# A state-space layer's scan: a decay factor computed ahead into a borrowed bank, transposes for VectorE put first, and a residual sum moved to VectorE

## Chip, cores and metric

One core of a Trainium2 chip. The metric is the time of one execution of the whole kernel on the device, in microseconds (us); the figure compared is the median over runs.

## What is computed

The kernel is one layer with a Mamba-like mixer and a mixture of experts. Input x is 8 sequences of 1024 tokens with 256 channels; the mixer has 512 inner channels and 16 states per channel.

```python
u, res = split(x @ W_in); u = silu(conv3(u))
dt, B, C = split(u @ W_x)
delta = softplus(dt @ W_dt + b_dt)
h = exp(delta * A) * h + delta * u * B      # scan over tokens, 16 states
y = (sum over states of h * C) + u * D_param
x = layernorm(x + (y * silu(res)) @ W_out)
x = layernorm(x + ffn(x))                   # top-2 of 8 experts
```

The change touches the mixer and its layer norm alone. Everything is float32 there.

## The kernel before

**Tiling.** The mixer (`attention`) works in 16 chunks of 512 tokens, two to a sequence; chunk numbers below count from 0. Channels lie on the 128 partitions in 4 tiles (t), so a chunk has 16 states times 4 tiles = 64 **slots**, slot = 4n + t. In every slot ScalarE computes the decay factor `da` = exp(delta * A) for 128 x 512 into one of two PSUM banks (L428; t even to one, t odd to the other) and VectorE scans it with `dbu` (L534) into `hst`. GpSimd makes `dbu` = (delta u) times B for a whole state, 128 x 2048, once in four slots (L349), into one of three buffers. ScalarE writes `da` of a slot only once the scan two slots before is done, since it has two banks. Odd chunks, which continue a sequence, start each scan from `carry`.

**After the scan of a state** TensorE transposes it (`turn`, L619), 128 tokens at a time: token blocks 0 and 1 through the single bank `hd`, which VectorE multiplies by C and adds to `yacc` (`add_state`, L512), after the scans of t = 1 and t = 3; blocks 2 and 3 through the single bank `w2`, which ScalarE scales by C into `hTC` (`scale_state`, L416), and which TensorE transposes back into accumulation banks (`accumulate`, L628). All of this is done while the next state is scanned, part of it in the state after that. TensorE's order in the four slots of a state is: turn block 2, turn block 0, turn block 3, turn block 1, with accumulations after the second and the fourth (L655 to L662).

**The projections share one ring of two banks**, `gen`. A table, `FILL_AT`, gives each fill's bank and the slots at which TensorE writes its parts; `READ_AT` gives the slot at which ScalarE reads it. They are: `r` (gate, 4 fills of 2 parts), `u` (convolution, 4 of 6 parts), `xd`, `cT`, `d`, `ud` for the next chunk; `C`, `o`, `xt`, `lg` to close the chunk before. `o0` and `o1` are the output projection plus the residual: for two token blocks each, four products with `w_out` and a fifth with the identity that adds `x_rows` (L592, L594). ScalarE reads them into `resid` with a row sum beside (L401), then takes the squares' sum (`STATS_AT`, L479), GpSimd makes `rstd` and `shift` with small operations at n = 11 (L317 to L324), and ScalarE normalises at slots 45 to 49 (L488).

**Order.** Every engine's order is written out by hand in slots; each waits in its own order on counting semaphores. At slot 19 ScalarE runs `SILU_AT`: a table load, SiLU of `u` and of the gate (128 x 2048 each), and a load of the exp table (L451 to L454). GpSimd multiplies by the gate in two halves (`GATE_AT`, before `dbu` of n = 4 and of n = 5, L313); `o0` and `o1` wait for these. `o1` alone is written ahead of the slot's turn (`BEFORE_TURN`, slot 20). Stages -2, -1 and 16 of the same code fill and empty the pipeline: chunk 0 has nothing to close, chunk 15 has nothing of a next chunk to prepare, and stage 16 only closes.

After the mixer come routing, the experts and a last normalisation, in which VectorE takes row statistics with `bn_stats` (L1526) and `bn_aggr`.

## Time and profile before

| | us |
|---|---|
| median of 3 runs | 2740.91 |
| lowest, highest | 2738.28, 2741.33 |
| the profiled execution: time | 2734.82 |
| the profiled execution: span | 2733.0 |
| PE busy | 2380.6 (87%) |
| DVE busy | 2104.4 (77%) |
| POOL busy | 1796.5 (66%) |
| ACT busy | 1769.6 (65%) |

The span runs from the first to the last instruction. PE is TensorE (matmuls; PEld its weight loads), DVE VectorE, ACT ScalarE, POOL GpSimd, SP SyncE, which issues DMAs. The mixer's chunks fill the time from 87 to about 1802 us; the busy shares above are means over it and over the experts' part, in which TensorE and others have other limits. An engine's idle time counts only on the path that sets the end, so the chunks are read by themselves. Times in a timeline are from the span's start; in brackets stands the idle time before an instruction and what ended it.

### The profile page before, as it was taken

The page shows a single profiled execution, that of the slowest core. Times are in us where ns is not written, and L with a number is a line of the kernel's source. Part 1 is how long each engine was busy: PE and PEld are TensorE (multiplying, and loading weights), DVE is VectorE, ACT ScalarE, POOL GpSimd, SP SyncE. Part 2 cuts the span into 40 slices and gives each one's busy share as a digit, 9 for nine tenths or more (in the row PEclk, how much of TensorE's full clock was granted, in tenths as well). Part 3 has the DMA queues.
Part 4 walks back from the last instruction along what each step waited for, and adds up shares of the span by engine and source line. Part 5 has one row for each costly group of instructions (what it writes and reads, how often), then busy time and mean ns, then how long its engine had stood idle before and what let it go on. Part 6 is the DMA issues. An engine that isn't in the chain of part 4 may idle for free. (4 is left out here: it accounts for less than half of the span.)

```text
span 2733.0 us, 44490 instructions
## 1 busy us (share of the span) xinstructions
PE 2380.6 (87%) x14216; PEld 1854.8 (68%) x14216; DVE 2104.4 (77%) x2764; ACT 1769.6 (65%) x3135; POOL 1796.5 (66%) x845
## 2 busy tenths in 40 slices
PE   7799999999998999998999997654899999999991
PEld 2466666756666667566666665544799989989991
DVE  0698888988988988989889889958476567567644
ACT  3688878887887887888878888733243344334434
POOL 0787877887888789778788788822164345425524
PEclk9999999999999999999999999975899999999996
DMA  2111211121121111111212111120122221323116
GB/s 69 39 48 55 70 56 63 57 64 61 55 65 54 63 55 63 63 55 55 71 47 63 55 62 63 47 77 23 44 67 53 72 67 34 84 59 82 34 19 253
DMA packets 84393, 169.79 MB, mean 62 GB/s; under 512 B 8480, under 2 KB 52000, under 8 KB 84144
## 3 DMA queue, kind: packets, MB, share of 16 engines
q1 hardware_dynamic: 68784, 145.72, 15.7%
q0 software_dynamic: 15360, 20.98, 4.5%
q8 instruction: 128, 2.10, 0.3%
q14 instruction: 121, 0.99, 0.1%
HBM read 130.49 MB, written 36.18 MB: 61 GB/s over the span
## 5 line engine op out<-in xcount | busy, mean ns | idle before, releaser
L349 POOL TENSOR_TENSOR dbu<-du,b_all 128x2048 f32<-128x2048 f32 x256 | 1161.7, 4545 | 166.4 <-DVE hst L534 166.3
L428 ACT ACTIVATE da<-delta,a_neg 128x512 f32<-128x512 f32 x1024 | 705.7, 691 | 255.6 <-DVE hst L534 249.4
L534 DVE TENSOR_TENSOR_SCAN hst<-da,dbu 128x512 f32<-128x512 f32 x512 | 600.3, 1207 | 131.6 <-ACT da L428 129.1
L534 DVE TENSOR_TENSOR_SCAN hst<-da,carry,dbu 128x512 f32<-128x512 f32 x512 | 630.8, 1267 | 53.6 <-ACT da L428 49.0
L619 PEld LDWEIGHTS w<-ident,hst 128*128 128x128 f32 x2048 | 232.5, 141 | 417.9 <-ACT hTC L416 270.0
L619 PE MATMUL w<-ident,hst 128*128 128x128 f32 x2048 | 324.4, 281 | 193.8 <-ACT hTC L416 166.6
L1424 PE MATMUL gu<-x_part,w_part 128*128 128x384 f32 (+1 forms) x2304 | 485.6, 359 | 4.9 <-ACT w_part L1320 3.2
L1424 PEld LDWEIGHTS gu<-x_part,w_part 128*128 128x128 f32 x2304 | 403.5, 189 | 35.3 <-DVE silu L1278 3.6
L512 DVE SCALAR_TENSOR_TENSOR yacc<-hd,c_tok,yacc 128x512 f32<-128x512 f32 x512 | 374.8, 732 | 66.0 <-PE hd L619 64.2
L557 PE MATMUL gen<-xT,w_u 128*128 128x512 f32 x768 | 394.3, 604 | 14.3 <-DVE w_u L497 12.7
L416 ACT ACTIVATE hTC<-w,c_tok 128x512 f32<-128x512 f32 x512 | 346.0, 676 | 9.1 <-PE w L619 9.1
L1361 ACT ACTIVATE silu<-gu 128x384 f32<-128x384 f32 (+1 forms) x192 | 101.3, 528 | 374.6 <-PE gu L1424 374.6
L619 PEld LDWEIGHTS hd<-ident,hst 128*128 128x128 f32 x2048 | 247.0, 142 | 137.6 <-issue 126.4
L1278 DVE TENSOR_TENSOR silu<-silu,gu 128x384 f32<-128x384 f32 (+1 forms) x192 | 114.5, 596 | 270.3 <-ACT silu L1361 267.9
L619 PE MATMUL hd<-ident,hst 128*128 128x128 f32 x2048 | 314.0, 276 | 0.7
L628 PE MATMUL acc<-ident,hTC 128*128 128x128 f32 x2048 | 310.0, 274 | 0.0
L1156 POOL DMA_INDIRECT xg<-x_dram,token x80 | 83.5, 1043 | 277.9 <-DVE token L1227 255.9
L1441 PE MATMUL dn<-w_part,hid_part 128*128 128x256 f32 x1920 | 257.9, 281 | 4.9 <-ACT eo L1340 4.9
L1441 PEld LDWEIGHTS dn<-w_part,hid_part 128*128 128x128 f32 x1920 | 251.3, 188 | 12.8 <-ACT eo L1340 6.8
L628 PEld LDWEIGHTS acc<-ident,hTC 128*128 128x128 f32 x2048 | 242.2, 142 | 0.0
L1151 POOL TENSOR_TENSOR w_part<-w_raw,w_mask 128x512 fp32r<-128x512 f32 x84 | 119.7, 1526 | 109.5 <-DVE w_mask L1242 109.5
L1166 POOL DMA_INDIRECT acc_dram<-eo,token x80 | 128.4, 1605 | 74.9 <-issue 42.4
(197 smaller groups left out, 2913.2 us busy)
## 6 DMA issues: line engine op xcount, KB each, us to landing
b_all<-b_rows SPq DMA_DIRECT2D x128, 512.0 KB, 3.6
xT<-in_xT SPq DMA_DIRECT2D x16, 514.0 KB, 4.9
x_rows<-in_x SPq DMA_DIRECT2D x16, 512.0 KB, 4.9
x_dram<-x SPq DMA_DIRECT2D x16, 512.0 KB, 3.1
acc_dram<-x SPq DMA_DIRECT2D x16, 512.0 KB, 5.1
w_raw<-in_wg SPq DMA_DIRECT2D x8, 1024.0 KB, 5.0
w_raw<-in_wu SPq DMA_DIRECT2D x8, 1024.0 KB, 8.0
w_raw<-in_wd SPq DMA_DIRECT2D x8, 1024.0 KB, 12.5
```

The lines of the kernel that those rows point to most:

```text
L349: nc.gpsimd.tensor_tensor(dbu[DBU[n]][:], du[parity][:], b_n, ALU.mult).then_inc(dbu_ready, 1)
L416: nc.scalar.activation(hTC[(2 * n + i) % 4][:], w2_bank[:], ACT.Copy, scale=c_tok[parity][:, LB + i, RANK + NST + n:RANK + NST + n + 1]).t ...
L428: nc.scalar.activation(da_bank[t % 2][:], delta[parity][:, t, :], ACT.Exp, scale=a_neg[:, t, n:n + 1]).then_inc(da_ready, 1)
L512: nc.vector.scalar_tensor_tensor(out=yacc[parity][:, l, :], in0=hd_bank[:], scalar=c_tok[parity][:, l, RANK + NST + n:RANK + NST + n + 1], ...
L534: nc.vector.tensor_tensor_scan(hst[DBU[n]][:, t, :], da_bank[t % 2][:], dbu[DBU[n]][:, t, :], initial, ALU.mult, ALU.add).then_inc(scanned, 1)
L557: last = nc.tensor.matmul(bank[:], w_u[:, tap, k, j * P:(j + 1) * P], xT[:, k, tap:tap + CL], start=part == 0, stop=part == parts - 1)
L619: last = nc.tensor.transpose(bank[:, t * P:(t + 1) * P], hst[DBU[n]][:, t, l * P:(l + 1) * P], ident[:])
L628: last = nc.tensor.matmul(acc_bank[i][:, t, :], hTC[(2 * n + i) % 4][:, t * P:(t + 1) * P], ident[:], start=False, stop=n == NST - 1, is_t ...
L1151: nc.gpsimd.tensor_tensor(parts[1], raw, mask_of(w, p, F32), ALU.subtract).then_inc(w_low, 1)
L1166: nc.gpsimd.indirect_dma_start(out=acc_d, out_offset=bass.IndirectOffsetOnAxis(ap=token[par][:, s:s + 1], axis=0), in_=eo[:, s, :], in_off ...
L1424: last = nc.tensor.matmul(gu_bank[n % 2][i][:, 0:width(n)], gu_part[wp][:, i, kk, f * P:(f + 1) * P], x_part[xp][:, kk, tokens_of(j)], sta ...
L1441: last = nc.tensor.matmul(dn_bank[s // SJ][:, s % SJ, :], hid_part[hp][:, h % HS, s * P:(s + 1) * P], down_part[wp][:, f, :], start=f == 0 ...
```

## The change

- **The early factor.** `da` of slot 20 is computed by ScalarE at slot 17, behind its other work there, into ring bank 1 instead of an own bank; VectorE scans slot 20 out of that bank. `da` of slot 22 then waits for the scan of slot 18 alone.
- **Ring bank 1** is free for it because `o1` is moved from slot 20 to slots 21 and 22, behind the turns and behind the scan of slot 20; the first part of `u0` goes from slot 24 to slot 25.
- **Turn order.** TensorE turns blocks 0, 2, 1, 3 (for state 4: 0, 1, 2, 3) instead of 2, 0, 3, 1. ScalarE's scalings, and with them the seeds and reads of the accumulation banks, go a slot or two later; both accumulations now come a state later, after the second and the fourth turn. VectorE's check that `hst` is free is now on block 3 (`w2_ready`).
- **`o0` goes to VectorE.** TensorE leaves out the two identity products for it; VectorE adds `x_rows` to the bank (blocks 2, 3), takes `bn_stats` and `bn_aggr`. This, and both `add_state` of state 4, stand behind the scan of slot 20. ScalarE no longer reads `o0` nor squares its blocks; `o1`'s stay, with statistics at slot 25.
- **GpSimd** has six small operations at n = 11 instead of four; its gate multiplies go to n = 5 and n = 6. The load of `x_rows` waits for `shift_ready` instead of the read of `o1`.

```diff
+VECTOR_READ = ("o0",)
+EARLY_SLOT, EARLY_AT, EARLY_BANK, EARLY_STATE = 20, 17, 1, 4
...
-           "o0": (0, 14, 15, 16, 17, 18), "o1": (1, 20, 20, 20, 20, 20), "xd": (0, 22, 23, 24, 25),
-           "u0": (1, 24, 25, 26, 27, 29, 30), ...
+           "o0": (0, 14, 15, 16, 17), "o1": (1, 21, 21, 21, 22, 22), "xd": (0, 22, 23, 24, 25),
+           "u0": (1, 25, 26, 27, 29, 30, 30), ...
...
-BEFORE_TURN = ("o1",)
+BEFORE_TURN = ()
-SEED_AT, ACC_READ_AT = (6, 8), (5, 7)
-SILU_AT, STATS_AT, EXP_AT, LN_AT, NORM_AT = 19, (22, 24), (41, 42), (43, 44), (45, 46, 48, 49)
-GATE_AT, SMALL_AT, ADD_AT, DU_AT = {4: 1, 5: 0}, 11, 14, 15
+SEED_AT, ACC_READ_AT = (8, 10), (7, 9)
+SILU_AT, STATS_AT, EXP_AT, LN_AT, NORM_AT = 19, 25, (41, 42), (43, 44), (45, 46, 48, 49)
+GATE_AT, SMALL_AT, ADD_AT, DU_AT = {5: 1, 6: 0}, 11, 14, 15
...
+        late = [x for x in same if FILL_AT[x][1] > EARLY_SLOT]
+        if self.main and FILL_AT[name][0] == EARLY_BANK and name == late[0]:
+            pe.wait_ge(scanned, self.c * SLOTS + EARLY_SLOT + 1)
...
+    def da_bank_free(self, slot):
+        return self.c * SLOTS + slot - (3 if slot == EARLY_SLOT + 2 else 1)
...
                         if s.close:
-                            sp.wait_ge(ring_read, o1_read)
+                            sp.wait_ge(shift_ready, shifted)
...
-                        wait_over(act, scanned, c * 64 + slot - 1)
-                        nc.scalar.activation(da_bank[t % 2][:], delta[parity][:, t, :], ACT.Exp,
-                                             scale=a_neg[:, t, n:n + 1]).then_inc(da_ready, 1)
-                    if t == 2 and s.state_before(n, 1) is not None:
+                        if slot != EARLY_SLOT:
+                            wait_over(act, scanned, s.da_bank_free(slot))
+                            nc.scalar.activation(da_bank[t % 2][:], delta[parity][:, t, :], ACT.Exp,
+                                                 scale=a_neg[:, t, n:n + 1]).then_inc(da_ready, 1)
+                    if t == 3 and s.state_before(n, 1) is not None:
...
-                    if t == 0 and s.state_before(n, 2) is not None:
+                    if t == 1 and s.state_before(n, 2) is not None:
...
+                    if slot == EARLY_AT and s.main:
+                        en, et = EARLY_SLOT // DT, EARLY_SLOT % DT
+                        wait_over(act, ring_read, s.early_bank_free())
+                        nc.scalar.activation(gen_bank[EARLY_BANK][:], delta[parity][:, et, :], ACT.Exp,
+                                             scale=a_neg[:, et, en:en + 1]).then_inc(da_ready, 1)
...
+            def sum_rows(s):
+                dve.wait_ge(rows_loaded, c * 16)
+                dve.wait_ge(ring_full, s.nth_full("o0") + 1)
+                wait_over(dve, x1_ready, c * LT - LT)
+                for l in O_BLOCKS[0]:
+                    nc.vector.tensor_tensor(resid[:, l, :], gen_bank[FILL_AT["o0"][0]][:, l % 2 * DM:(l % 2 + 1) * DM],
+                                            x_rows[:, l, :], ALU.add).then_inc(rows_summed, 1)
+            def measure_rows(s):
+                dve.wait_ge(rows_summed, c * 2)
+                for l in O_BLOCKS[0]:
+                    nc.vector.bn_stats(stats[:, l - 2, :], resid[:, l, :]).then_inc(rows_measured, 1)
...
-                        dve.wait_ge(da_ready, c * 64 + slot + 1)
+                        dve.wait_ge(da_ready, c * 64 + DA_ORDER.index(slot) + 1)
...
-                                dve.wait_ge(hd_ready, c * (NST * LB) + LB * done + LB)
+                                dve.wait_ge(w2_ready, c * (NST * LB) + LB * done + LB)
...
-                    if t % 2 == 1 and s.state_before(n, 1) is not None:
+                    if t % 2 == 1 and n != EARLY_STATE + 1 and s.state_before(n, 1) is not None:
                         add_state(s, s.state_before(n, 1), t // 2)
+                    if slot == EARLY_SLOT:
+                        if s.main:
+                            add_state(s, s.state_before(n, 1), 0)
+                        if s.close:
+                            sum_rows(s)
+                            measure_rows(s)
+                            dve.wait_ge(rows_measured, c * 2)
+                            wait_over(dve, shift_ready, c - 1)
+                        if s.main:
+                            add_state(s, s.state_before(n, 1), 1)
+                        if s.close:
+                            aggregate_rows(s)
...
-                        turn(one, (2, 0, 3, 1)[q])
-                    if q == 1 and two is not None:
-                        accumulate(two, 1)
-                    if q == 3 and one is not None:
-                        accumulate(one, 0)
+                        turn(one, ((0, 1, 2, 3) if n == EARLY_STATE + 1 else (0, 2, 1, 3))[q])
+                    if q % 2 == 1 and two is not None:
+                        accumulate(two, q // 2)
```

## Rows read from the trace of the kernel before

**Rows 1.** Stretches, chunk 6 and all: us, busy PE PEld DVE ACT POOL, PEclk, DMA, GB/s.

```profile
733.36:841.79 108.43, 98.34 (x576) 68.95 (x575) 94.41 (x97) 88.98 (x154) 91.01 (x40) 1.00 0.19 60
86.98:1805.00 1718.02, 1521.38 (x9000) 1081.81 (x8998) 1534.78 (x1536) 1396.64 (x2390) 1398.99 (x504) 0.99 0.18 58
```

**Rows 2.** VectorE's waits: who waited, for whom, us in total, times, longest.

```profile
DVE hst L534 <- ACT da L428: 178.1, 85, 71.1
...
DVE yacc L512 <- PE hd L619: 64.2, 99, 1.9
```

**Rows 3.** Timeline of VectorE in chunk 6, slots 18 to 36: start, us, engine, line.

```profile
759.60 2.32 DVE L534 TENSOR_TENSOR_SCAN hst<-da,dbu 128x512 f32<-128x512 f32 x2
...
761.85 0.72 DVE L512 SCALAR_TENSOR_TENSOR yacc<-hd,c_tok,yacc 128x512 f32<-128x512 f32 x1
...
767.16 2.34 DVE L534 TENSOR_TENSOR_SCAN hst<-da,dbu 128x512 f32<-128x512 f32 x2 [4.59 <-ACT da L428]
...
771.83 1.22 DVE L534 TENSOR_TENSOR_SCAN hst<-da,dbu 128x512 f32<-128x512 f32 x1 [0.56 <-ACT da L428]
...
777.05 0.75 DVE L512 SCALAR_TENSOR_TENSOR yacc<-hd,c_tok,yacc 128x512 f32<-128x512 f32 x1 [0.27 <-PE hd L619]
...
781.18 0.75 DVE L512 SCALAR_TENSOR_TENSOR yacc<-hd,c_tok,yacc 128x512 f32<-128x512 f32 x1 [1.14 <-PE hd L619]
...
788.22 2.33 DVE L534 TENSOR_TENSOR_SCAN hst<-da,dbu 128x512 f32<-128x512 f32 x2
...
794.49 2.34 DVE L534 TENSOR_TENSOR_SCAN hst<-da,dbu 128x512 f32<-128x512 f32 x2 [0.41 <-POOL carry L346]
```

**Rows 4.** Timeline of ScalarE in chunk 6, slots 19 and 20.

```profile
759.86 1.28 ACT L451 ACT_TABLE_LOAD   x1
...
766.18 0.69 ACT L428 ACTIVATE da<-delta,a_neg 128x512 f32<-128x512 f32 x1
766.81 0.67 ACT L416 ACTIVATE hTC<-w,c_tok 128x512 f32<-128x512 f32 x1
```

**Rows 5.** Groups by line and form: ScalarE's reads and squares, VectorE's nearest kinds.

```profile
L401 ACT ACTIVATE resid<-gen 128x256 f32<-128x256 f32 x64 | 23.3, 369 | 10.0 <-PE gen L594 10.0
...
L479 ACT ACTIVATE x<-resid,minus_mean 128x256 f32<-128x256 f32 x64 | 32.0, 501 | 1.0
...
L1278 DVE TENSOR_TENSOR silu<-silu,gu 128x512 f32<-128x512 f32 x64 | 43.9, 686 | 103.1 <-ACT silu L1361 102.5
...
L1526 DVE BATCH_NORM_STATS2 stats<-rows 128x6 f32<-128x256 f32 x64 | 23.2, 404 | 19.3 <-DMA rows<-acc_dram 19.3
```

**Rows 6.** Timeline of TensorE in chunk 6, slot 20.

```profile
761.70 1.89 PE L592 MATMUL gen<-w_out,yT 128*128 128x256 f32 x8
...
763.43 0.59 PE L594 MATMUL gen<-x_rows,ident 128*128 128x256 f32 x2
...
767.53 0.66 PE L619 MATMUL w<-ident,hst 128*128 128x128 f32 x4 [1.35 <-ACT hTC L416]
768.02 0.60 PE L619 MATMUL hd<-ident,hst 128*128 128x128 f32 x4
```

**Rows 7.** Timeline of GpSimd in chunk 6, the multiply for n = 6.

```profile
760.62 4.57 POOL L349 TENSOR_TENSOR dbu<-du,b_all 128x2048 f32<-128x2048 f32 x1
```

**Rows 8.** Timeline of VectorE in chunk 6, slots 59 and 61.

```profile
832.82 0.75 DVE L512 SCALAR_TENSOR_TENSOR yacc<-hd,c_tok,yacc 128x512 f32<-128x512 f32 x1 [0.84 <-PE hd L619]
...
836.82 0.75 DVE L512 SCALAR_TENSOR_TENSOR yacc<-hd,c_tok,yacc 128x512 f32<-128x512 f32 x1 [1.00 <-PE hd L619]
```

**Rows 9.** Timeline of VectorE in chunk 5, slot 3.

```profile
630.87 0.75 DVE L512 SCALAR_TENSOR_TENSOR yacc<-hd,c_tok,yacc 128x512 f32<-128x512 f32 x1 [0.79 <-PE hd L619]
```

**Rows 10.** Timeline of VectorE in chunk 15, slot 21.

```profile
1733.71 0.75 DVE L512 SCALAR_TENSOR_TENSOR yacc<-hd,c_tok,yacc 128x512 f32<-128x512 f32 x1 [1.92 <-PE hd L619]
```

**Rows 11.** Timeline of VectorE and GpSimd in the last normalisation.

```profile
2698.42 0.72 DVE L1526 BATCH_NORM_STATS2 stats<-rows 128x6 f32<-128x256 f32 x2
2698.66 0.55 POOL L1557 TENSOR_SCALAR rows<-rows,rstd,shift 128x256 f32<-128x256 f32 x1
```

More of the change, by code:

```diff
@@ L82, in nth_full, with base_read, wait_bank, early_bank_free @@
         return self.base() + sorted(self.fills, key=lambda x: FILL_AT[x][-1]).index(name)
+    def base_read(self):
+        k = len(VECTOR_READ)
+        if not isinstance(self.c, int):
+            return self.c * (len(FILL_AT) - k) + (36 - len(FILL_AT) + k)
+        return self.base() - max(0, self.c - 1) * k
     def nth_read(self, name):
-        return self.base() + sorted(self.fills, key=lambda x: READ_AT[x]).index(name)
-    def read_before(self, name):
+        read = [x for x in self.fills if x not in VECTOR_READ]
+        return self.base_read() + sorted(read, key=lambda x: READ_AT[x]).index(name)
+    def wait_bank(self, pe, name, ring_read, rows_summed, scanned):
         same = [x for x in self.fills if FILL_AT[x][0] == FILL_AT[name][0]]
         k = same.index(name)
-        return self.nth_read(same[k - 1]) + 1 if k else self.base()
+        if k and same[k - 1] in VECTOR_READ:
+            pe.wait_ge(rows_summed, self.c * 2)
+        else:
+            wait_over(pe, ring_read, self.nth_read(same[k - 1]) + 1 if k else self.base_read())
+        late = [x for x in same if FILL_AT[x][1] > EARLY_SLOT]
+        if self.main and FILL_AT[name][0] == EARLY_BANK and name == late[0]:
+            pe.wait_ge(scanned, self.c * SLOTS + EARLY_SLOT + 1)
+    def early_bank_free(self):
+        used = [x for x in self.fills if FILL_AT[x][0] == EARLY_BANK and x in READ_AT and READ_AT[x] <= EARLY_AT]
+        return self.nth_read(max(used, key=lambda x: READ_AT[x])) + 1 if used else self.base_read()
+    def da_bank_free(self, slot):
+        return self.c * SLOTS + slot - (3 if slot == EARLY_SLOT + 2 else 1)
     def state_before(self, n, back):
@@ L207, in attention @@
         gated = sem("gated")
+        rows_summed = sem("rows_summed")
+        rows_measured = sem("rows_measured")
+        moments_ready = sem("moments_ready")
         mean_ready = sem("mean_ready")
@@ L467, in chunk @@
                                              ).then_inc(soft_step, 1)
-                    if slot in STATS_AT and s.close:
-                        j = STATS_AT.index(slot)
-                        act.wait_ge(ring_read, s.nth_read(f"o{j}") + 1)
-                        if j == 0:
-                            wait_over(act, x1_stored, c * 32 - 32)
-                        pair = slice(O_BLOCKS[j][0], O_BLOCKS[j][-1] + 1)
+                    if slot == STATS_AT and s.close:
+                        act.wait_ge(ring_read, s.nth_read("o1") + 1)
+                        wait_over(act, x1_stored, c * 32 - 32)
+                        pair = slice(O_BLOCKS[1][0], O_BLOCKS[1][-1] + 1)
                         nc.scalar.activation(minus_mean[:, pair], row_sum[:, pair], ACT.Copy,
                                              scale=-1.0 / DM).then_inc(mean_ready, 1)
-                        act.wait_ge(mean_ready, c * 2 + (j - 1))
-                        for l in O_BLOCKS[j]:
+                        act.wait_ge(mean_ready, c)
+                        for l in O_BLOCKS[1]:
                             last = nc.scalar.activation(x1[:, l, :], resid[:, l, :], ACT.Square,
@@ L515, in add_state, with aggregate_rows @@
                     in1=yacc[parity][:, l, :], op0=ALU.mult, op1=ALU.add).then_inc(summed, 1)
+            def sum_rows(s):
+                c = s.c
+                dve.wait_ge(rows_loaded, c * 16)
[5 more added lines that the diff above has]
+            def measure_rows(s):
+                c = s.c
+                dve.wait_ge(rows_summed, c * 2)
+                for l in O_BLOCKS[0]:
+                    nc.vector.bn_stats(stats[:, l - 2, :], resid[:, l, :]).then_inc(rows_measured, 1)
+            def aggregate_rows(s):
+                for l in O_BLOCKS[0]:
+                    nc.vector.bn_aggr(mean_var[:, l - 2, :], stats[:, l - 2, :]).then_inc(moments_ready, 1)
             def chunk(s):
@@ L533, in chunk @@
                         initial = carry[:, n, t:t + 1] if parity == 1 else 0.0
[L534 removed]
+                        decay = gen_bank[EARLY_BANK] if slot == EARLY_SLOT else da_bank[t % 2]
+                        nc.vector.tensor_tensor_scan(hst[DBU[n]][:, t, :], decay[:], dbu[DBU[n]][:, t, :],
                                                      initial, ALU.mult, ALU.add).then_inc(scanned, 1)
[L536 removed]
+                    if t % 2 == 1 and n != EARLY_STATE + 1 and s.state_before(n, 1) is not None:
                         add_state(s, s.state_before(n, 1), t // 2)
+                    if slot == EARLY_SLOT:
[10 more added lines that the diff above has]
+                            aggregate_rows(s)
             over_chunks(dve, chunk)
@@ L550, in fill @@
                 if part == 0:
-                    wait_over(pe, ring_read, s.read_before(name))
+                    s.wait_bank(pe, name, ring_read, rows_summed, scanned)
                 what, j = name.rstrip("0123"), int(name[-1]) if name[-1].isdigit() else 0
@@ L585, in fill @@
                         pe.wait_ge(gated, c * 2 + (j - 1))
-                    if name == "o0" and part == 0:
+                    if name == "o1" and part == 0:
                         pe.wait_ge(rows_loaded, c * 16)
-                    for l, t in [(l, t) for l in O_BLOCKS[j] for t in range(DT + 1)][2 * part:2 * part + 2]:
+                    terms = DT if name in VECTOR_READ else DT + 1
+                    for l, t in [(l, t) for l in O_BLOCKS[j] for t in range(terms)][2 * part:2 * part + 2]:
                         acc = bank[:, l % 2 * DM:(l % 2 + 1) * DM]
                         if t < DT:
-                            nc.tensor.matmul(acc, yT[:, t, l * P:(l + 1) * P], w_out[:, t, :], start=t == 0, stop=False)
+                            last = nc.tensor.matmul(acc, yT[:, t, l * P:(l + 1) * P], w_out[:, t, :], start=t == 0,
+                                                    stop=t == terms - 1)
                         else:
```

30 lines of the change are left out of this document (19 added, 11 removed), and 2 rows, old and new, of the table FILL_AT.

## The prediction

> **What bounds the kernel now.** I read the stretches first. Over the mixer's chunks VectorE is busy 1534.8 of 1718 us; in chunk 6, which I take as the pattern, 94.4 of 108.4 us, GpSimd 91.0, ScalarE 89.0 and TensorE 98.3, whose ends are modelled [rows 1]. Four engines are nearly full, and VectorE's scans carry the order, so what counts is VectorE's idle time: 14.0 us a chunk. Its waits name two causes: decay factors (178.1 us in 85 waits, 71.1 of it the one before the first scan, so 107 in the chunks) and the transposed state in `hd` (64.2 us in 99) [rows 2]. The timeline shows where. The pair of slots 18 and 19 starts at 759.60, its `add_state` at 761.85, and slot 20 only at 767.16, after 4.59 us for its factor; then come smaller waits for factors (0.56) and, as TensorE has fallen behind, for `hd` (0.27, 1.14) [rows 3]. ScalarE's timeline gives the reason: from the load of the SiLU table at 759.86 to the next factor at 766.18 it is 6.32 us in the SiLU block [rows 4]. The two banks hold factors for two slots, 2.3 us of scans.
>
> **The change, part by part,** walked through chunk 6, on its clock.
>
> *ScalarE into the block.* The extra Exp at slot 17 costs 0.63 (766.18 to 766.81 [rows 4]); I price it at nothing, since ScalarE then waits for scan 16 anyway; were it busy there, 0.63. The scaling moved from slot 18 to slot 19, 0.57, lies ahead of the block. So the block starts at about 760.43, and the next factor, now slot 21's, starts 6.32 later, 766.75, and is ready at 767.4.
>
> *VectorE in that time.* The last `add_state` frees it at 762.5. Slot 20 has its factor: 1.2, to 763.7. First `add_state` of state 4, 0.65. Two adds of 128x256 from PSUM: no row shows them; half of a 128x512 one (0.69) is 0.34, a whole one the upper end [rows 5]; I take 0.38 as overhead doesn't halve, 0.75 together. Two `bn_stats`, 0.72 for two back to back [rows 11], 0.40 each by the mean [rows 5]: 0.72. Second `add_state` 0.65. Two aggregations, no row here: between nothing and a `bn_stats` each; 0.2 together. Hand-overs of VectorE to itself: 0.2. End 766.9 (766.4 to 768.2 at the bounds). Slot 21 waits 0.5 and starts at 767.45. The new work of 1.9 us lies wholly beside the block; without the block it would cost 1.9.
>
> *Slots 21 to 27.* Scans 21, 22, 23 follow at 1.15 each with factors in time, as ScalarE has lost the reads of `o0` (0.37 each and accumulator reads) and two squares (0.50 each) [rows 5], 2.6 us with their small companions. Slot 24 starts at 771.0; before, the factor of slot 23 alone came at 771.83 [rows 3]. Now `o1` presses: TensorE wrote it in the shadow from 761.70; four of its products take 1.73 (761.70 to 763.43), so 0.43 each and 4.3 in all [rows 6]. Now it starts behind the second turn, at 765.3 (`add_state` ends 764.3, a turn and an accumulation under 0.49 each: 767.53 to 768.02, after a wait [rows 6]), has 6 products done at 767.9, waits for ScalarE's scaling (768.1), and is full at 770.3. ScalarE reads it and takes its statistics between the factors of slots 24, 25 and 26: VectorE waits 0.45 and 0.65. Then slots 26, 27 and an `add_state`: slot 28 starts at 778.0. Before, the wait of 1.14 ended at 781.18, and slot 28 followed at 781.85 [rows 3]. `o0` without its two identity products saves TensorE 0.86.
>
> *Slots 28 to 35.* TensorE has the rest of `u0`, `cT` and `d0` and is a turn ahead of what it was, because `hd` now comes first. By its sum (a convolution part, 512 columns, twice a 256-column product: 0.86; a turn 0.44, my estimate for one that runs on, below the 0.49 above) `hd` for slot 33 comes at 787.5 while VectorE is there at 786.5: a wait of 1.0. Slot 32 starts at 784.2 (before 788.22), slot 36 at 791.2 (before 794.49, behind a wait of 0.41) [rows 3]. **Gain to here 3.3 us**, of 7.7 that slots 20 to 31 waited.
>
> *Slots 36 to 63.* ScalarE is full from slot 38 to 49 (softplus, normalisation); the order of scalings changes, the sum doesn't: +0.4. From slot 46 TensorE is full with `u2`, `u3`, `ud`, `xt` and `lg`. The waits for `hd` at slots 59 and 61, 0.84 and 1.00 [rows 8], and two or three small ones go, 2.7 us, as the turns for VectorE come a slot sooner. In return slot 60 waits for the last turn of state 13 in `w2` at TensorE's slot 59 (this is the new check; nothing but that scan is queued behind it): 0.55 by my sum, and 0.2 elsewhere. **Gain 2.0 and 0.4.** At the start of odd chunks the wait of 0.79 [rows 9] goes, 0.4 on average.
>
> *Priced at nothing.* GpSimd's gate multiplies a state later: the multiply for n = 6 runs to 765.2 [rows 7], and slot 24 comes at 771; `o0`'s start at slot 14 gets its gate 0.1 before its turn (0.5 if I read that wrong). GpSimd's two added small operations, at most the 0.55 of a larger one each [rows 11], lie in an idle stretch of it before n = 12. The load of `x_rows` is held on SP's queue till GpSimd's small operations at n = 11; behind it stands only the load of B for n = 14, which waits for the multiply of n = 11 anyway.
>
> *Sum.* A chunk: 3.3 + 0.4 + 2.0 + 0.4 = 6.1. The walk leaves out small hand-overs (0.04 to 0.1 each, some nine): I take **5.2** for each of chunks 1 to 14, 73 us. Chunk 0 has the block but no `o`: 4. Chunk 15 has no block: 1.9 of new work, against a wait of 1.92 for `hd` behind `o1` [rows 10], which goes: nothing. The closing stage saves the identity products, 1. Sum 78. The profiled execution, 2734.8 (1.8 above its span), would become 2657; the median of the runs lies 6.1 above it, so 2663.
>
> **A rule against the change.** In the last normalisation two `bn_stats` beside a GpSimd operation on SBUF (0.55 us) take 0.72 [rows 11], so 0.36 each, no more than the mean of all [rows 5]. The Trainium skill, SBUF — State Buffer, section "SBUF: two separate sides", says that VectorE in a two-port mode or with two SBUF inputs and GpSimd lock a shared port pair, and the loser waits for the whole instruction. By that rule `bn_stats` would only be held if it ran in such a mode, and the trace speaks against it. As a mechanism here: GpSimd's multiply from 760.62 runs to 765.19 [rows 7] and the next follows at once; `bn_stats` at 765.1 and its second would each wait out a 4.55 us multiply, 9 us less the 0.5 of slack: a loss of some 3 us a chunk.
>
> **Rivals.**
> - *TensorE takes over.* Its 98 us of busy time [rows 1] leave little; `o1`'s 4.3 us move out of the idle shadow into the stretch where it is behind. If that stretch and slot 60 lose another 2.2 us, 3 remain: 42 + 3 = 45 us, **2696**. For it: `hd` waits already stand there. Against: ScalarE's late scaling held it before (1.35 [rows 6]), and that no longer delays `hd`. 17%.
> - *The hand-written order was looser than I take it,* VectorE near its floor: idle outside the new waits gone, 7 us a chunk, 98 + 5: **2638**. 13%.
> - *Slower:* the place is slot 21. If `o1` counts whole (4.3), the new VectorE work counts whole (1.9) and the checks on `w2` at slots 60 and 4 cost one turn and one convolution part each (2.6), 8.8 stand against 7.2 recovered (4.59, 0.56, 0.27, 1.14 and some): +1.6 times 14, **2763**. It decides if less than 4.59 of the block is covered. 4%. The port lock, +3 times 15, gives 2786: 2%.
> - *The early factor doesn't come early:* scan 18 now waits for it too (20 factors counted). If ring bank 1 is not free at slot 17, the block's wait only moves; what is left is the turn order, some 2 us: **2710**. `r3` is read two slots before, so hardly. 4%.
>
> **Numbers.** My forecast has 60%, 2663; its own range is 2645 to 2685. To leave out no more than 2 in 10 the range is 2638 to 2700: it takes in TensorE's case and the better one. A difference below 0.2%, 5.5 us, can't be told here. Faster 0.92, same 0.02 (between the cases), slower 0.06.
>
> **What would show it.** `da` for slot 20 before that of slot 18; slot 20 without wait; 0.4 to 0.9 us before slot 21; `bn_stats` at 0.36; `hd` waits in total below 25 us; a wait of about 0.5 before slot 60; chunk 6 about 103 us long. Wrong would be: `bn_stats` over 1 us, a wait before slot 20, `hd` waits of over 2 us in slots 26 to 35, or the wait at slot 60 over 1.5.

## The result, and the profile after

The changed kernel took **2718.09 us**, median of four runs (2715.93 to 2720.49), against 2741.12 for four runs of the kernel before (2738.28 to 2741.41): a ratio of 0.9918 [0.9906, 0.9930]. It is 23 us faster. The forecast was 78 us, and its range ended at 2700: the sign came true, the size did not.

The profiled execution took 2720.49 us, span 2718.7. The profile splits it at two rows of VectorE's timeline: the first scan of chunk 0, and the maximum over the router's logits, where the mixer is over. The first fence is the kernel after, the second the kernel before.

```profile
88.33 2.34 DVE L599 TENSOR_TENSOR_SCAN hst<-da,dbu 128x512 f32<-128x512 f32 x2 [72.51 <-ACT da L467]
...
1811.93 0.69 DVE L1023 TENSOR_REDUCE row_max<-logits 128x64 f32<-128x512 f32 x1 [16.89 <-PEq L149]
```

```profile
1830.39 0.69 DVE L947 TENSOR_REDUCE row_max<-logits 128x64 f32<-128x512 f32 x1 [28.53 <-PEq L123]
```

Before, the mixer took 1743.4 us (1830.39 less the start at 86.98, the first stretch of [rows 1]), after 1723.6: 19.8 us less, where 78 were forecast. Chunks 1 to 14 gained 20.8 us, 1.5 each instead of 5.2; chunk 0 lost 0.6, chunk 15 and the closing stage 0.4. What follows, the experts' part, ran 902.6 us before and 906.8 after in the profiled executions, though its code is the same. The profiled execution of before lay 6.3 below its median, so the medians differ by more than the two profiles do; for the mixer I go by the profiles, for the whole by the medians.

Chunk 6 in the stretches, and VectorE's waits over the whole program (for [rows 1] and [rows 2]):

```profile
728.59:836.08 107.49, 99.52 (x572) 69.75 (x572) 96.53 (x103) 88.12 (x145) 92.03 (x42) 0.98 0.19 60
```

```profile
DVE hst L599 <- ACT da L467: 142.1, 120, 72.5
...
DVE yacc L554 <- PE hd L697: 47.2, 58, 1.7
```

VectorE has 2.1 us more work in the chunk (96.5 against 94.4 [rows 1]) and is idle 11.0 instead of 14.0. The granted clock of the chunk is 0.98 instead of 1.00. The waits for factors fell by 36 us in all, those for `hd` by 17; they were to fall below 25. VectorE's timeline tells which went and which came (slots 20 to 37; before in [rows 3]):

```profile
757.45 1.23 DVE L599 TENSOR_TENSOR_SCAN hst<-gen,dbu 128x512 f32<-128x512 f32 x1
...
759.23 0.76 DVE L566 TENSOR_TENSOR resid<-gen,x_rows 128x256 f32<-128x256 f32 x2
760.02 0.75 DVE L574 BATCH_NORM_STATS2 row_stats<-resid 128x6 f32<-128x256 f32 x2
760.97 0.75 DVE L554 SCALAR_TENSOR_TENSOR yacc<-hd,c_tok,yacc 128x512 f32<-128x512 f32 x1 [0.20 <-DVE row_stats L574]
761.64 0.24 DVE L579 BATCH_NORM_AGGREGATE row_mean_var<-row_stats 128x2 f32<-128x6 f32 x2
762.41 3.53 DVE L599 TENSOR_TENSOR_SCAN hst<-da,dbu 128x512 f32<-128x512 f32 x3 [0.54 <-ACT da L467]
766.86 1.22 DVE L599 TENSOR_TENSOR_SCAN hst<-da,dbu 128x512 f32<-128x512 f32 x1 [0.92 <-ACT da L467]
768.40 1.22 DVE L599 TENSOR_TENSOR_SCAN hst<-da,dbu 128x512 f32<-128x512 f32 x1 [0.32 <-ACT da L467]
770.62 0.75 DVE L554 SCALAR_TENSOR_TENSOR yacc<-hd,c_tok,yacc 128x512 f32<-128x512 f32 x1 [1.00 <-PE hd L697]
...
775.03 0.75 DVE L554 SCALAR_TENSOR_TENSOR yacc<-hd,c_tok,yacc 128x512 f32<-128x512 f32 x1 [1.41 <-PE hd L697]
775.70 2.33 DVE L599 TENSOR_TENSOR_SCAN hst<-da,dbu 128x512 f32<-128x512 f32 x2
...
784.41 1.22 DVE L599 TENSOR_TENSOR_SCAN hst<-da,dbu 128x512 f32<-128x512 f32 x1 [1.13 <-ACT da L467]
...
786.92 2.34 DVE L599 TENSOR_TENSOR_SCAN hst<-da,dbu 128x512 f32<-128x512 f32 x2 [0.45 <-ACT da L467]
...
790.14 2.34 DVE L599 TENSOR_TENSOR_SCAN hst<-da,dbu 128x512 f32<-128x512 f32 x2 [0.23 <-ACT da L467]
```

Slot 20 comes without a wait, the new work follows it, and slot 21 waits 0.54. Chunk 6 began at 733.36 before and at 728.59 now, so 4.77 is added to read these times on the clock of the prediction. The start of a slot, forecast and measured: 21: 767.45 and 767.18; 24: 771.0 and 771.63; 28: 778.0 and 780.47; 36: 791.2 and 794.91 (794.49 before). To slot 24 the walk holds within 0.6 us. From there on another 3.1 us are lost against it, in the waits of 0.32, 1.00 and 1.41 at slots 25 to 27 and in 1.13, 0.45 and 0.23 at slots 33, 34 and 36.

What TensorE did meanwhile (slots 20 to 24; before in [rows 6]), and the stretches around it, where the granted clock is the third column from the end:

```profile
757.61 0.66 PE L697 MATMUL hd<-ident,hst 128*128 128x128 f32 x4 [0.55 <-DVE yacc L554]
759.38 0.66 PE L697 MATMUL hd<-ident,hst 128*128 128x128 f32 x4 [1.12 <-DVE yacc L554]
759.87 0.73 PE L706 MATMUL acc<-ident,hTC 128*128 128x128 f32 x4
760.39 3.49 PE L669 MATMUL gen<-w_out,yT 128*128 128x256 f32 x8
...
766.84 1.06 PE L642 MATMUL gen<-u,w_x 128*48 128x512 f32 x2
```

```profile
757.00:759.00 2.00, 0.71 (x5) 0.42 (x4) 2.00 (x3) 2.00 (x2) 2.00 (x1) 1.00 0.87 186
759.00:760.40 1.40, 1.02 (x9) 1.02 (x10) 1.36 (x5) 1.38 (x2) 1.40 (x1) 0.93 0.00 0
760.40:762.00 1.60, 1.60 (x5) 1.33 (x5) 1.28 (x5) 1.59 (x2) 1.60 (x3) 0.50 0.00 0
762.00:764.20 2.20, 2.20 (x8) 1.76 (x8) 1.79 (x2) 2.10 (x4) 2.20 (x1) 0.63 0.00 0
764.20:766.00 1.80, 1.80 (x12) 1.60 (x11) 1.74 (x2) 0.87 (x3) 0.88 (x1) 1.00 0.00 0
```

With `o1` gone from the shadow of the block, TensorE waits 0.55 and 1.12 us for VectorE; from 757 to 759 it is busy 0.71 of 2.00 us. Then the granted clock is 0.50, 1.2 instead of 2.4 GHz, for some 3.4 us by these stretches, and it is there that `o1` is written: its first four products, eight instructions, take 3.49 us, where before four took 1.89 at the full clock [rows 6]. Eight chunks of the kernel after (1, 2, 4, 6, 7, 12, 13, 15) have this at slot 20. Of the closing chunks of the kernel before none has. The idle time alone does not settle it: chunk 8 of the kernel after has the same two waits, and stayed at the full clock.

```profile
974.11 0.66 PE L697 MATMUL hd<-ident,hst 128*128 128x128 f32 x4 [1.12 <-DVE yacc L554]
...
975.04 1.89 PE L669 MATMUL gen<-w_out,yT 128*128 128x256 f32 x8
```

```profile
971.74:973.74 2.00, 0.70 (x5) 0.42 (x4) 2.00 (x3) 2.00 (x2) 2.00 (x1) 1.00 0.56 156
...
975.14:976.74 1.60, 1.60 (x9) 1.42 (x8) 1.27 (x5) 1.59 (x2) 1.60 (x3) 1.00 0.00 0
```

Counted from their own start, both chunks reach slot 23 within 0.01 us of each other; chunk 8 reaches slot 24 sooner by 1.0 and slot 36 by 1.5. Against the kernel before it gains 1.07 us to slot 36, where chunk 6 loses 0.42: that is the price of one half clock.

The waits at slots 33 and 34 are read on ScalarE and TensorE:

```profile
783.20 0.60 ACT L409 ACTIVATE u_raw<-gen 128x512 f32<-128x512 f32 x1 [2.02 <-PE gen L634]
783.69 0.69 ACT L467 ACTIVATE da<-delta,a_neg 128x512 f32<-128x512 f32 x1
```

```profile
781.20 1.88 PE L634 MATMUL gen<-xT,w_u 128*128 128x512 f32 x4
```

ScalarE takes its work in order. It stands 2.02 us at its read of `u0`, whose last parts TensorE does only at 781.20 to 783.1, and the factor for slot 33 is queued behind that read. Chunk 14 has no `u0`, and ran at the full clock at slot 20: there the gain over the kernel before, counted from the chunk's start, is 3.0 us at slot 24, 2.15 at slot 28 and 2.16 at slot 36, and 3.15 at its end. In chunk 6 the same points give 1.98, 1.38, -0.42 and 0.94.

### The profile page after: what moved, and what is told of

Its sections match the earlier page's. It is cut to its first block and busy times, and to the rows that moved or that the text cites. A ratio compares the mean times of both kernels' runs of the same rounds, so it can differ in the third digit from the quotient of the medians.

```text
span 2718.7 us, 44389 instructions
## 1 busy us (share of the span) xinstructions
PE 2395.2 (88%) x14152; PEld 1856.4 (68%) x14152; DVE 2138.2 (79%) x2860; ACT 1757.7 (65%) x2991; POOL 1801.6 (66%) x877
## 3 DMA queue, kind: packets, MB, share of 16 engines
q14 instruction: 131, 1.07, 0.1%
## 5 line engine op out<-in xcount | busy, mean ns | idle before, releaser
L467 ACT ACTIVATE da<-delta,a_neg 128x512 f32<-128x512 f32 x1008 | 689.3, 691 | 132.4 <-DVE hst L599 118.0
L599 DVE TENSOR_TENSOR_SCAN hst<-da,dbu 128x512 f32<-128x512 f32 x504 | 592.5, 1212 | 110.2 <-ACT da L467 108.3
L599 DVE TENSOR_TENSOR_SCAN hst<-da,carry,dbu 128x512 f32<-128x512 f32 x504 | 621.1, 1271 | 39.9 <-ACT da L467 33.7
L697 PEld LDWEIGHTS hd<-ident,hst 128*128 128x128 f32 x2048 | 238.5, 142 | 328.1 <-DVE yacc L554 156.8
L697 PE MATMUL hd<-ident,hst 128*128 128x128 f32 x2048 | 323.5, 281 | 124.2 <-DVE yacc L554 105.6
L554 DVE SCALAR_TENSOR_TENSOR yacc<-hd,c_tok,yacc 128x512 f32<-128x512 f32 x512 | 375.9, 734 | 52.3 <-PE hd L697 47.2
L697 PEld LDWEIGHTS w<-ident,hst 128*128 128x128 f32 x2048 | 240.8, 143 | 208.0 <-ACT hTC L454 104.1
```

Of the source, the lines that this page charges most:

```text
L467: nc.scalar.activation(da_bank[t % 2][:], delta[parity][:, t, :], ACT.Exp, scale=a_neg[:, t, n:n + 1]).then_inc(da_ready, 1)
L554: nc.vector.scalar_tensor_tensor(out=yacc[parity][:, l, :], in0=hd_bank[:], scalar=c_tok[parity][:, l, RANK + NST + n:RANK + NST + n + 1], ...
L599: nc.vector.tensor_tensor_scan(hst[DBU[n]][:, t, :], decay[:], dbu[DBU[n]][:, t, :], initial, ALU.mult, ALU.add).then_inc(scanned, 1)
L697: last = nc.tensor.transpose(bank[:, t * P:(t + 1) * P], hst[DBU[n]][:, t, l * P:(l + 1) * P], ident[:])
```

## The experiments

"Mixer" is, as above, the time from the first scan to the maximum over the logits, from the profiled execution; the gain in a chunk is against the kernel before from the chunk's start on. The first group is four kernels; the kernel before took 2740.26 us beside them (13 runs), beside the second group 2742.33 (7), and beside the third, when the experts' part of every profiled kernel was some 36 to 40 us longer, 2778.83 (13). So across groups I compare ratios and mixers. Each mixer time comes from one execution, and the mean granted clock of the kernel after lay between 0.954 and 0.957 in its four runs, so a difference of a few us between two mixers is weak evidence by itself. The gains at a slot of chunk 6 repeat to a few hundredths wherever the clock is the same.

| kernel | median us | ratio to before | mixer us |
|---|---|---|---|
| after | 2718.09 | 0.9918 [0.9906, 0.9930] | 1723.6 |
| e1_zeros | 2719.76 | 0.9929 [0.9912, 0.9945] | 1713.3 |
| e2_o1first | 2710.50 | 0.9893 [0.9877, 0.9910] | 1713.4 |
| e3_o1cut | 2694.44 | 0.9828 [0.9812, 0.9844] | 1699.0 |
| e4_order | 2734.07 | 0.9979 [0.9970, 0.9989] | 1737.6 |
| e5_due | 2702.67 | 0.9855 [0.9839, 0.9872] | 1708.5 |
| e6_early | 2720.17 | 0.9919 [0.9902, 0.9935] | 1724.0 |
| e7_unroll | 2685.79 | 0.9795 [0.9778, 0.9811] | 1692.4 |
| e8_spread | 2700.50 | 0.9850 [0.9834, 0.9867] | 1702.2 |
| e9_before_unroll | 2761.80 | 0.9938 [0.9921, 0.9955] | 1730.2 |
| e10_spread_unroll | 2711.30 | 0.9757 [0.9740, 0.9773] | 1677.9 |
| e11_o1late | 2777.48 | 0.9988 [0.9977, 0.9999] | 1746.7 |
| e12_stats | 2751.61 | 0.9903 [0.9886, 0.9919] | 1720.0 |

### e1: TensorE kept busy in the shadow

In slot 20 of chunks 0 to 14, four products with zeros ahead of the first turn and ten behind it, added to a bank that they don't change.

```diff
+def fill_time(s, count):
+    for _ in range(count):
+        nc.tensor.matmul(acc_bank[1][:, 0, :], zeros[:], ident[:], start=False, stop=False,
+                         is_transpose=True, skip_group_check=True)
...
+if slot == EARLY_SLOT and s.main and s.front:
+    fill_time(s, 4)
 turn(one, ...)
```

> The changed kernel (2718 us) with 14 transposes of a zero tile, added to an accumulation bank, in the two places of slot 20 where TensorE stood idle (4 ahead of the first turn, 10 behind it); the results are the same. Theory A, the granted clock: in the changed kernel TensorE works at 0.50 to 0.63 for 3.4 us behind these idle places, just where o1 is written, and is the bound up to slot 33; with the filler the half clock goes, slots 21 to 33 shorten by 1.0 to 1.7 us a chunk, 2695 to 2704 us. Rival B, only the place of o1 counts and its end is covered by ScalarE: the clock comes back to 1.00 and the time stays at 2715 to 2720. Rival C: the filler delays the second turn and with it slot 21: over 2722.

The half clock at slot 20 was gone from all closing chunks (from chunk 15 too, which has no added products), and the mixer took 10.3 us less, with more work on TensorE than before the edit. In chunk 6 the gain at slot 36 rose from -0.42 to 1.06, what chunk 8 has without the edit. The time of the whole did not follow: the experts' part took 913.1 us instead of 906.8, and the median stayed at 2719.76. So the time alone would read as rival B, and theory A's 2695 to 2704 was missed; the mixer speaks for A's mechanism. The half clock was a cost of the change; it was not the largest.

### e2: a first part of o1 ahead of the turn

```diff
-BEFORE_TURN = ()
+BEFORE_TURN = (("o1", 0),)
```

(the part named is issued before the turn of its slot, the other four behind, as in the change)

> The changed kernel with the first of o1's five parts written ahead of the second turn of slot 21, in TensorE's idle time, the rest behind it. Theory A: o1 ends 0.9 us sooner by place, and if the shorter idle time also keeps the clock, 1.7 more; 2692 to 2708 us. Rival B (o1's end is covered): 2718. Rival C: the second turn comes some 0.3 us later and slot 21 with it: 2720 to 2724.

The same 10.2 us of the mixer, without the added work, and here 7.6 of them show in the time: 2710.50, just above theory A's range. In chunk 6 every start of a scan is that of e1 within 0.02 us, so the earlier place of the first part brought nothing there beyond the clock. Only chunks 1 and 13 still had the half clock at slot 20. Chunk 6 starts 5.7 us sooner here, so the stretch that was at 0.50 lies at about 755 to 758.5, and the clock is 1.00:

```profile
753.00:757.00 4.00, 3.73 (x20) 3.02 (x20) 3.22 (x9) 3.97 (x4) 4.00 (x3) 1.00 0.04 15
757.00:759.00 2.00, 1.67 (x10) 1.55 (x11) 2.00 (x2) 1.90 (x4) 2.00 (x1) 1.00 0.00 0
```

The gain in chunk 6 is 2.99 at slot 24, close to the forecast's 3.3 at slot 36; but 0.90 at slot 34. So a second loss lies behind.

### e3: a smaller o1

```diff
 for l, t in [(l, t) for l in O_BLOCKS[j] for t in range(terms)][2 * part:2 * part + 2]:
+    if name == "o1" and 0 < t < DT:
+        continue
```

> The changed kernel without six of the ten products of o1 (terms 1 to 3 of both blocks), so the output projection of two token blocks is incomplete. It prices TensorE's time in slots 21 to 33. If TensorE is the bound there, as theory A has it, 2.6 us at full clock and more at half come off each chunk until another engine takes over: 2675 to 2690 us. If ScalarE or VectorE is the bound there (rival B): 2712 to 2718.

With six products (2.6 us) of `o1` left out the mixer took 24.6 us less than after, 14.4 less than e2; the time, 2694.44, is 4 us above theory A's range. The gain at slot 28 is 4.17, where e2 has 2.87. So TensorE's work in slots 21 to 27 is on the path, and half of what is taken off it there comes back. (It was on the path before the change too, by the waits of 0.27 and 1.14 for `hd` [rows 3].) Yet the loss of 2 us between slots 32 and 34 is the same:

```profile
769.93 1.22 DVE L599 TENSOR_TENSOR_SCAN hst<-da,dbu 128x512 f32<-128x512 f32 x1 [1.13 <-ACT da L467]
...
772.45 2.34 DVE L599 TENSOR_TENSOR_SCAN hst<-da,dbu 128x512 f32<-128x512 f32 x2 [0.45 <-ACT da L467]
```

A TensorE that is 2.6 us less loaded in front of slot 28 leaves this wait at 1.13 and 0.45, to the hundredth. So it does not come from `o1`; the next pair of runs moves `u0`.

### e4 and e6: the change in steps

e4 is the kernel before with the new order of turns, scalings and gates alone; e6 adds the early factor to it, with the later places of `o1` and `u0`, and leaves `o0` as it was, read by ScalarE, with its identity products.

```diff
-SEED_AT, ACC_READ_AT = (6, 8), (5, 7)
+SEED_AT, ACC_READ_AT = (8, 10), (7, 9)
...
-turn(one, (2, 0, 3, 1)[q])
+turn(one, (0, 2, 1, 3)[q])
...
-if q == 1 and two is not None:
-    accumulate(two, 1)
-if q == 3 and one is not None:
-    accumulate(one, 0)
+if q % 2 == 1 and two is not None:
+    accumulate(two, q // 2)
```

> The kernel before (2741 us) with the turn order, the scalings, accumulations, seeds, gate multiplies and the check on w2 of the change, and nothing else: no early factor, o0 still with ScalarE. By the prediction's terms (2.4 us in slots 46 to 63, 0.4 at the chunk's start): 2700 to 2705 us. By the two traces (2.2 gained late, some 0.7 lost at the hand-over between chunks): about 2720. Rival: the order alone gives nothing, 2738 to 2744.

> The kernel of e4_order (2734 us) with the early factor, o1 at slots 21 and 22 and u0 a slot later, so the change without the move of o0 to VectorE: ScalarE still reads o0 and squares its blocks, TensorE still adds its rows. Theory A: the early factor moves o1 into TensorE's full stretch and ScalarE is loaded as before, so most of what is gained at slot 20 is lost by slot 34; 2722 to 2732 us, and the move of o0 is worth the rest to 2718. Rival: the early factor carries all of the gain, 2715 to 2721.

The order alone is worth 5.8 us of the mixer (its ten runs lie between 2729 and 2740, between its two cases), the early factor 13.6 more, and `o0` on VectorE 0.4. That last part saved ScalarE 2.0 us a chunk (the two reads and two squares of `o0`, 767.99 to 768.71 and 769.89 to 771.13 before) and TensorE 0.86, and brought nothing by itself. But e6 has the half clock in slot 20 of no closing chunk; on TensorE it differs from the kernel after by the identity products of `o0` (0.86 us), and of the two waits of chunk 6 at slot 20 it has only the second, 1.02. In e1 and e2, where `o0` is on VectorE and the clock stays up, the mixer is 10.7 and 10.6 us below e6. So this part of the change is worth about 10 us and gave them back, by the clock as far as e1 and e2 show.

### e5 and e8: u0 later

Both build on e2. e5 does the last part of `u0` a slot later and reads it a slot later, and moves the `d` blocks by a slot too:

```diff
-"u0": (1, 25, 26, 27, 29, 30, 30), "cT": (0, 28), "d0": (0, 31), "d1": (1, 33), "d2": (0, 35),
+"u0": (1, 25, 26, 27, 29, 30, 31), "cT": (0, 28), "d0": (0, 32), "d1": (1, 34), "d2": (0, 36),
```

e8 spreads `u0` among the `d` blocks and reads it at slot 36 instead of 32:

```diff
-"u0": (1, 25, 26, 27, 29, 30, 30), "cT": (0, 28), "d0": (0, 31), "d1": (1, 33), "d2": (0, 35),
+"u0": (1, 25, 27, 29, 30, 32, 34), "cT": (0, 28), "d0": (0, 31), "d1": (0, 33), "d2": (0, 35),
```

> The kernel of e2_o1first (2710.5 us) with the last part of u0 at slot 31 instead of twice at slot 30, its read at slot 33, and d0 to d3 filled a slot later (32, 34, 36, 38; d0 and d1 read at 34 and 36). In chunk 6 of the changed kernel ScalarE stands 2.02 us for the end of u0 and VectorE then 1.13 and 0.45 us for the factors of slots 33 and 34. Theory A (TensorE is full there, the read only shows it): the wait moves a slot on, at most 0.5 us a chunk gained, 2703 to 2712 us. Rival D (the two parts at slot 30 and the early read are the cause themselves): 1.0 to 1.5 us a chunk, 2689 to 2697 us.

> The kernel of e2_o1first (2710.5 us) with the parts of u0 spread over slots 25 to 34 and read at slot 36, d1 moved to bank 0 at slot 33. TensorE's work is the same, but less of it lies in slots 25 to 32 and more where TensorE stands idle behind slot 33. Theory A (TensorE is the bound in slots 25 to 33 alone): the waits for hd at slots 25 and 27 stay (0.95, 1.41), those of 1.13 and 0.45 at slots 33 and 34 go: 2688 to 2700 us. If ScalarE is the bound behind slot 33: 2705 to 2711.

e5 took 4.9 us off e2's mixer, and its time lies at the edge of theory A: in chunk 6 the gain at slot 34 rose from 0.90 to 2.54, and of the wait a part, 0.86, moved on to slot 35. e8 took 11.2 off. Slot 33 now follows slot 32 without a wait, and what is left stands at slots 34 and 36 (the rows are slots 32, 34 and 36 with the one behind each):

```profile
768.60 2.32 DVE L599 TENSOR_TENSOR_SCAN hst<-da,dbu 128x512 f32<-128x512 f32 x2
...
772.41 2.34 DVE L599 TENSOR_TENSOR_SCAN hst<-da,dbu 128x512 f32<-128x512 f32 x2 [0.53 <-ACT da L467]
...
775.97 2.34 DVE L599 TENSOR_TENSOR_SCAN hst<-da,dbu 128x512 f32<-128x512 f32 x2 [0.58 <-ACT da L467]
```

In the time e8 stands at 2700.50, 10 us below e2. So the second loss is the place of `u0`, which reaches VectorE by ScalarE's read of it ahead of a factor. Chunk 14, which has no `u0`, shows no loss there either. Both runs move TensorE's parts together with the read, so what the later read alone would give was not tried.

### e7 and e9: no loop over the chunks

A third loss lies at the start of odd chunks, where the loop's body begins anew. VectorE waits there before slot 0 and, in chunk 5, again at slots 3 and 4 ([rows 9] has the one at slot 3 before):

```profile
621.58 2.46 DVE L599 TENSOR_TENSOR_SCAN hst<-da,carry,dbu 128x512 f32<-128x512 f32 x2 [2.02 <-ACT da L467]
...
627.96 0.75 DVE L554 SCALAR_TENSOR_TENSOR yacc<-hd,c_tok,yacc 128x512 f32<-128x512 f32 x1 [0.92 <-PE hd L697]
629.42 2.46 DVE L599 TENSOR_TENSOR_SCAN hst<-da,carry,dbu 128x512 f32<-128x512 f32 x2 [0.70 <-PE w L697]
```

Both kernels have the chunks of the loop written out, e7 the one after, e9 the one before.

```diff
-with eng.Fori(0, (CHUNKS - 4) // 2) as i:
-    emit(Stage(i * 2 + 1, 1, True, True, True, True))
-    emit(Stage(i * 2 + 2, 0, True, True, True, True))
+for c in range(1, CHUNKS - 3):
+    emit(Stage(c, c % 2, True, True, True, True))
```

> The changed kernel (2718 us) with the twelve chunks of its loop written out, same instructions, no branch. In the trace VectorE waits 1.9 to 2.0 us at slot 0 of every second chunk (1.34 before the change), and TensorE's half clock stands at these places too. Theory E: the branch costs VectorE these 2 us six times and the half clock behind it another 1.6 in some: 2695 to 2706 us. Rival: the wait is for the state's last scalings, not for the branch; 2715 to 2718.

> The kernel before (2741 us) with the same twelve chunks written out. Written out, the changed kernel fell by 32 us, to 2685.8. Theory E1: the loop cost both kernels about the same, then this one falls by 20 to 30 us, 2711 to 2721, and the change is worth about as much without the loop as with it, 25 to 35 us. Rival E2: the change had made the branch dearer (ScalarE's last scaling now stands right ahead of it, the check on w2 behind it); then this one falls by 5 to 15 us only, 2726 to 2736, and the change without the loop is worth 40 to 50.

The loop costs the kernel before 13.2 us of its mixer and the kernel after 31.2. Without loops the change is worth 37.8 us of the mixer (1730.2 to 1692.4), with them 19.8, near the lower end of rival E2's 40 to 50. With the loop VectorE waits at slot 0 of chunks 3, 5, 7, 9 and 11, 1.17 to 1.34 us before and 1.87 to 2.10 after; written out, at slot 0 of none, in e7 and in e9. In e7 the start of chunk 7 runs through (slot 0 is the second row):

```profile
818.98 0.72 DVE L553 SCALAR_TENSOR_TENSOR yacc<-hd,c_tok,yacc 128x512 f32<-128x512 f32 x1
819.63 2.45 DVE L598 TENSOR_TENSOR_SCAN hst<-da,carry,dbu 128x512 f32<-128x512 f32 x2
```

e7 also has the half clock at slot 20 only in chunks 1, 9 and 15 instead of eight, which by e1 and e2 is some 7 of these 31 us. Of the remainder, 24 us, the five waits at slot 0 are 10.0 (6.3 before); the rest was not traced wait by wait. The half clock at slot 0 or 1 of chunks 3, 5 and 9 stands in the kernel before as well; the kernel after has it in chunk 11 too, for 6.8 us. In e4, which has the new order and no early factor, the waits at slot 0 are 2.03 to 2.54 already: it is the order that makes them longer. By what engine was not tried.

### e10: both

e8 with the chunks written out.

> e8_spread (2700.5 us) with the twelve chunks written out. If the gains add up (32 us for the loop, of which some 8 were half clock that e8 had lost already): 2666 to 2678 us. Rival: they overlap, as both take the same waits away: 2680 to 2686.

The mixer is 1677.9 us, 65.5 less than that of the kernel before, and the ratio 0.9757 [0.9740, 0.9773]: some 67 us, faster than both kernels; against 2741 that ratio is 2674, within the range for gains that add up. Chunk 6 has gained 2.63 us at slot 36 (e8: 2.36), 4.49 at slot 63 (4.29) and 5.88 at its end, where e8 has 3.45 and e7 4.87. Against e9, the kernel before without the loop, it is 52.3 us of the mixer.

### e11: o1 spread over eight slots

As e10, but `o1` at slots 21 to 29 and read at 31, `u0` wholly behind it at 31 to 36, and all four `d` blocks in one bank.

> Written out, and o1's five parts spread over slots 21, 23, 25, 27, 29 (read at 31), u0 behind it at slots 31 to 36 (read at 38), xd and d all in bank 0. It takes TensorE's work out of slots 21 to 30, where theory A has it as the bound, and puts it into slots 31 to 38, where TensorE waits. Theory A: the waits of 0.95 and 1.41 us for hd at slots 25 and 27 go, another 1.0 to 2.0 us a chunk: 2645 to 2660 us. Rival: ScalarE, with the same reads later, or u1 behind d3 in bank 0 gives it back: 2665 to 2680.

A miss: the mixer took 1746.7 us, 68.8 more than e10. The gain in chunk 6 is 2.26 at slot 36 and -0.86 at slot 38, after a wait of 1.36 at slot 32 and one of 3.01 at slot 37, where the `d` blocks follow each other through one bank and `u0` comes in one piece; which of the two it is was not tried. Chunk 14 alone lost 8.0 against e10, with the half clock for 17 us. Of the waits that it was to remove, the one at slot 25 fell from 0.89 to 0.43, the one at slot 27 stayed, 1.46 for 1.50. What is taken out of one slot has to fit into another, and the granted clock was lower too (0.947 against 0.952 over the span).

### e12: small statistics

The statistics of `o0`'s rows leave out 248 of the 256 channels.

```diff
-nc.vector.bn_stats(stats[:, l - 2, :], resid[:, l, :]).then_inc(rows_measured, 1)
+nc.vector.bn_stats(stats[:, l - 2, :], resid[:, l, 0:8]).then_inc(rows_measured, 1)
```

> The changed kernel (2718 us) with bn_stats over 8 columns instead of 256, so the statistics of two token blocks are those of 8 channels. It takes 0.5 to 0.6 us of VectorE's new work a chunk away. If that work lies wholly beside ScalarE's SiLU block, as predicted, slot 21 waits that much longer and the time stays at 2715 to 2721; if it is on the path, 8 us less, 2708 to 2712.

```profile
758.38 0.24 DVE L574 BATCH_NORM_STATS2 row_stats<-resid 128x6 f32<-128x8 f32 x2
...
760.78 3.53 DVE L599 TENSOR_TENSOR_SCAN hst<-da,dbu 128x512 f32<-128x512 f32 x3 [1.06 <-ACT da L467]
```

Two `bn_stats` fell from 0.75 to 0.24 us, and the wait at slot 21 grew from 0.54 to 1.06, by just that much: the new work is hidden beside the block, as priced. The mixer took 1720.0, 3.6 less than after. The trace puts that to where the half clock fell and not to VectorE's work: at slot 20 it lies in six closing chunks instead of eight, chunks 6 and 7 have it no more, and the gain of chunk 6 at slot 36 is 1.07, that of e2 and of chunk 8 of the kernel after.

## Why the prediction was wrong in size

**What came true.** The early factor is scanned without a wait in every chunk, where 4.2 to 4.6 us stood before in chunks 0 to 14. The price of the new VectorE work: 0.76 for two adds (0.75 forecast), 0.75 for two `bn_stats` (0.72), 0.24 for two aggregations (0.2), 0.20 of hand-over (0.2); slot 21 waits 0.54 (0.5). The gain from slot 36 to 63 is 2.0 us in chunk 6 and in chunk 5 (-0.42 to 1.56, -0.12 to 1.90), where 2.4 was forecast; the new wait before slot 60 of chunk 6 is 0.63 (0.55). The moves on GpSimd and SP cost nothing that a wait shows. The rule on the shared port pair did not bite: `bn_stats` took 0.37 each with GpSimd's multiply beside it. By the Trainium skill, SBUF — State Buffer, section "SBUF: two separate sides", that is what is expected of an operation outside its two conditions, and this trace agrees. None of the four signs of being wrong appeared: what failed was in none of them.

**The first failing step: "Slots 21 to 27" and "Slots 28 to 35", a gain of 3.3 us to slot 36.** Measured were -0.42 in chunk 6 and 1.06 with the clock kept up (e1). Of the 3.7 us that are missing, the half clock is 1.5; slots 32 to 36 lost 1.8 where 0.7 was forecast, 1.1; and 1.1 is missing at slot 32 already, at the full clock (2.87 of 4.0). Three things were wrong in it.
- `o1` was walked at 0.43 us a product. That price came from a time at which `o1` itself kept TensorE busy. Moved out, it left TensorE idle in the shadow, and in eight of the fifteen closing chunks the clock was at half when it was written: 3.49 us for four products instead of 1.89. e1 and e2: 10 us of the mixer.
- The walk let a late TensorE reach VectorE by `hd` alone. It also gets there by ScalarE, whose read of `u0` at slot 32 stands ahead of the factor for slot 33. The forecast had a wait for `hd` of 1.0 at slot 33; the real one was 1.13 and 0.45 for factors, and it stands even with `o1` shortened (e3). e8, with `u0` and its read later: 11 us of the mixer.
- The waits of 0.45 and 0.65 that the walk has between slots 24 and 28 were 0.32, 1.00 and 1.41, the last two for `hd`. The walk follows `o1` there, and names no price for the four parts of `xd`, which TensorE writes in the same slots at 0.99 each (766.84 to 767.83). At the full clock the two waits for `hd` are still 0.96 and 1.41 (e2). What in detail sets the second was not tried; it shrank only where `o1` was cut, to 0.59 in e3, and not where `o1` was spread, in e11. ScalarE's relief was sized at 2.6 us and is 2.0.

This is the first rival, "TensorE takes over", in its place, but larger than it was priced: it left 3 us a chunk, and 1.5 were measured. It should have had more than 17%, since TensorE's busy 98 of 108 us stood in the first row read; they became 99.5 of 107.5. Its mechanisms, the half clock and the queue of ScalarE, were not in it.

**The second failing step: "At the start of odd chunks the wait of 0.79 goes, 0.4 on average".** The waits there became larger, not smaller: 1.87 to 2.10 at slot 0 against 1.17 to 1.34, with 0.92 at slot 3 of chunk 5, where 0.79 was to go, and 0.70 at slot 4. The turn of the loop was no term of the sum. It costs 18 us of the mixer more than before (31.2 less 13.2, e7 against e9), some 7 of them by the half clock at slot 20.

**The third: chunk 0 (+4) and the closing (+1)** gave -0.6 and -0.4. In chunk 0 the half clock lay over slots 5 to 11, with waits of 1.68 and 0.93 for `hd` at slots 11 and 13; chunk 15 had it at slot 20 and lost 1.2 to slot 63, where e2, without it, gained 1.1. From there to the maximum e2 lost 2.3 and the kernel after gained 0.7; why was not tried.

In sum: 3.3 + 0.4 + 2.0 + 0.4 less hand-overs, 5.2, against 1.5 measured. Of the gap of 3.7 us a chunk, e2 returns 0.7 and e8 a further 0.8. Writing out the loop gives 24.3 us on top of e8, but 13.2 also to the kernel before, so 11.1 or 0.8 a chunk belong to the gap: 2.3 in all. The remaining 1.4 a chunk stays open. The waits for `hd` at slots 25 and 27 are still there in e8 and e10, and it may lie in them.

## What to carry to other kernels

Work that is moved out of an idle stretch is not only added where it goes: it takes away what kept the engine busy, and on TensorE the granted clock may then be at half just when the moved work runs, as in eight of fifteen chunks here. So a shadow is best left with a part of it in. When several engines are near full, walk the queue of each one: an engine that waits in order for one result holds back everything behind, so a late matmul reaches VectorE by way of ScalarE's reads too. And the turn of a hardware loop is a term of the sum, which a tighter order makes larger: 13 us before, 31 after.
